# A mixture-of-experts block in fp32r: the transposes of the next tile's rows move from the down-projection to the last up-projection chunk

## The reference

```python
w = weights[subjects]                           # one 64x64 map of 8 for each of 64 batches
xf = einsum('bct,bcd->bdt', x, w).reshape(-1, 512)         # 4096 tokens, 512 wide
probs = softmax(xf @ gate_w.T); top_p, top_i = top_k(probs, 2)     # 8 experts
h = silu(einsum('nc,efc->enf', xf, fc1)) * einsum('nc,efc->enf', xf, fc2)    # f: 352
out_e = einsum('enf,ecf->enc', h, proj)
y = einsum('ne,enc->nc', combine, out_e)        # combine holds top_p at top_i
shared = silu(xf @ shared_fc1.T) * (xf @ shared_fc2.T) @ shared_proj.T       # f: 1408
return x + y + sigmoid(xf @ shared_gate_w.T) * shared
```

## Time and profile before

| | |
|---|---|
| median of three runs | 1295.43 us (1293.08 to 1296.06) |
| profiled execution: span from first to last instruction | 1294.0 us |
| TensorE busy | 1277.8 us, 99% of the span |
| TensorE weight loads (PEld) | 1104.3 us, 85% |
| VectorE, ScalarE, GpSimd busy | 757.2, 442.1, 230.9 us |
| HBM traffic | 172 GB/s over the span |

### The profile page before, as it was taken

How to read it: one execution, slowest core, us unless ns; L and a number is a source line. 1 busy time by engine, 2 the same in 40 slices (tenths; PEclk the granted TensorE clock), 3 DMA queues, 4 the chain that set the end, 5 groups by cost and what they waited for, 6 DMA issues and landing times.

```text
span 1294.0 us, 20330 instructions
## 1 busy us (share of the span) xinstructions
PE 1277.8 (99%) x7150; PEld 1104.3 (85%) x7150; DVE 757.2 (59%) x1285; ACT 442.1 (34%) x744; POOL 230.9 (18%) x336
## 2 busy tenths in 40 slices
PE   6999999999999999999999999999999999999998
PEld 5888888888888989999999999998888888888886
DVE  5444443459645777777687677767535435445444
ACT  4323231121012666566566565555101101101100
POOL 4121220000001222212211221110122122122031
PEclk9999999999999999999999999999999999999999
DMA  9454544201235767777768766756152351351342
GB/s 317 125 196 144 203 126 163 106 33 66 98 124 186 273 248 257 267 260 261 264 238 279 269 224 242 254 212 220 60 163 60 103 162 48 114 162 43 120 130 65
DMA packets 84491, 222.72 MB, mean 172 GB/s; under 512 B 8578, under 2 KB 8706, under 8 KB 79458
## 3 DMA queue, kind: packets, MB, share of 16 engines
q1 hardware_dynamic: 73650, 186.77, 40.4%
q0 software_dynamic: 10800, 35.40, 10.0%
HBM read 169.97 MB, written 52.17 MB: 172 GB/s over the span
## 4 chain that ended last, share of the span: by engine, by line
PE 95%; DMA 2%; DVE 1%; issue 1%; SPq 1%; ACT 0%; POOLq 0%; POOL 0%; DVEq 0%
PE bank_h L644 60%; PE bank_o L644 29%; PE bank_t L634 2%; PE bank_t L644 2%; PE bank_t L591 1%; DMA rawp<-ewp 1%; PE bank_o L601 1%; PE bank_h L601 1%; DMA rawp<-swp 0%; DMA picked<-slot_rows,idx_stage 0%; PE bank_t L752 0%; DVE res L1333 0%; PE bank_h L853 0%; SPq L316 0%; DVE w_lo L1362 0%
## 5 line engine op out<-in xcount | busy, mean ns | idle before, releaser
L644 PE MATMUL bank_h<-x_hi,w_hi 128*128 128x256 f32 (+1 forms) x1480 | 499.6, 338 | 3.6 <-DVE x_lo L1370 2.8
L644 PE MATMUL bank_h<-x_hi,w_lo 128*128 128x256 f32 (+1 forms) x1480 | 493.3, 333 | 0.0
L644 PE MATMUL bank_h<-x_lo,w_hi 128*128 128x256 f32 (+1 forms) x1480 | 492.8, 333 | 0.0
L644 PEld LDWEIGHTS bank_h<-x_hi,w_hi 128*128 128x128 f32 x1480 | 273.4, 185 | 31.1 <-issue 4.7
L644 PEld LDWEIGHTS bank_h<-x_hi,w_lo 128*128 128x128 f32 x1480 | 273.3, 185 | 27.4
L644 PEld LDWEIGHTS bank_h<-x_lo,w_hi 128*128 128x128 f32 x1480 | 273.5, 185 | 26.4
L959 ACT ACTIVATE g_sb<-bank_h 128x512 f32<-128x512 f32 x88 | 52.6, 598 | 580.0 <-PE bank_h L644 580.0
L644 PE MATMUL bank_o<-wp_hi,h_hi 128*128 128x512 f32 (+1 forms) x565 | 229.4, 406 | 0.0
L1289 DVE TENSOR_TENSOR h_sb<-bank_h,g_sb 96x256 f32<-96x256 f32 (+1 forms) x184 | 101.3, 550 | 218.4 <-ACT g_sb L959 193.8
L644 PE MATMUL bank_o<-wp_lo,h_hi 128*128 128x512 f32 (+1 forms) x565 | 228.7, 405 | 0.0
L644 PE MATMUL bank_o<-wp_hi,h_lo 128*128 128x512 f32 (+1 forms) x565 | 227.5, 403 | 0.0
(11 more groups left out here) (154 smaller groups left out, 1134.3 us busy)
## 6 DMA issues: line engine op xcount, KB each, us to landing
raw<-ew SPq DMA_DIRECT2D x39, 1408.0 KB, 7.4
rawp<-ewp SPq DMA_DIRECT2D x39, 512.0 KB, 7.9
slot_rows<-res SPq DMA_DIRECT2D x32, 512.0 KB, 4.6
xt_in<-xf_transposed SPq DMA_DIRECT2D x15, 1024.0 KB, 8.3
picked<-x SPq DMA_DIRECT2D x32, 256.0 KB, 3.2
xf_rows<-rows SPq DMA_DIRECT2D x32, 256.0 KB, 3.3
res<-x SPq DMA_DIRECT2D x8, 1024.0 KB, 5.3
partial_rows<-res SPq DMA_DIRECT2D x8, 1024.0 KB, 4.2
```

The source lines that it names most:

```text
L644: mm = pe.matmul(dst, a, m, start=(first and i == 0), stop=(last and i == 2))
```

## The change

The eight (or four) transposes of the next tile's rows leave the down-projection. They stand in the last up chunk of the tile, one after every second pass from the second on. The wait for the gathered rows moves with them, to just ahead of that chunk. Nothing else changes: the queues of ScalarE, VectorE, GpSimd and SyncE are the same row by row. Single steps keep their transposes where they were.

```diff
--- before.py
+++ after.py
@@ -778,27 +778,36 @@
                         transpose_rows(ex, 0, k, rows[:, k, :])
                 shared_row(0, BLOCKS - 1, r)
 
-            def up_product(i, u, j, h, k, start, stop):
+            def up_product(i, u, j, h, k, start, stop, small=None):
 
                 f0, fn = FCH[j]
                 a = u * E_UP + k * 2 * F + h * F + f0
                 return product(bank_h[j][0:fn, h * TS:(h + 1) * TS], (w12_hi[:, a:a + fn], w12_lo[:, a:a + fn]),
-                               (x_hi[:, k, 0:TS], x_lo[:, k, 0:TS]), start, stop)
-
-            def whole_chunk(i, u, j):
+                               (x_hi[:, k, 0:TS], x_lo[:, k, 0:TS]), start, stop, small)
+
+            def whole_chunk(i, u, j, row_tiles=0):
                 at_least(pe, ex.h_mul, 3 * (i - 1) + j + 1)
                 for h in range(2):
                     for k in range(KC):
-                        m = up_product(i, u, j, h, k, k == 0, k == KC - 1)
+
+                        def small(pas, at=3 * (KC * h + k)):
+                            q, odd = divmod(at + pas, 2)
+                            if odd and q < row_tiles * KC:
+                                transpose_rows(ex, 2 * (i + 1), q // KC, rows[:, 2 * (1 - u) + q // KC, :], (q % KC,),
+                                               3 - row_tiles)
+
+                        m = up_product(i, u, j, h, k, k == 0, k == KC - 1, small)
                 m.then_inc(ex.h_full, 1)
 
-            def expert_stage1(i, u):
+            def expert_stage1(i, u, row_tiles=0, loaded=0):
                 pe.wait_ge(ex.x_lo, 2 * (i + 1))
                 pe.wait_ge(ex.w_lo, PIECES * i + KC)
                 for j in range(3):
-                    whole_chunk(i, u, j)
-
-            def expert_stage2(i, u, row_tiles):
+                    if j == 2 and row_tiles:
+                        pe.wait_ge(ex.rows_loaded[1 - u], loaded)
+                    whole_chunk(i, u, j, row_tiles if j == 2 else 0)
+
+            def expert_stage2(i, u):
 
                 pe.wait_ge(ex.w_lo, PIECES * (i + 1))
                 if isinstance(i, int) and i == 0:
@@ -812,22 +821,15 @@
                             fn = FCH[k][1]
                             w = slice(u * E_DOWN + k * C, u * E_DOWN + (k + 1) * C)
 
-                            def small(pas, at=3 * (2 * r + k)):
-                                q = at + pas
-                                if ks != (2,) and q < row_tiles * KC:
-                                    transpose_rows(ex, 2 * (i + 1), q // KC, rows[:, 2 * (1 - u) + q // KC, :], (q % KC,),
-                                                   3 - row_tiles)
-
                             m = product(bank_o[r][:, :], (h_hi[0:fn, k, c], h_lo[0:fn, k, c]),
-                                        (wp_hi[0:fn, w], wp_lo[0:fn, w]), k == 0, k == 2, small)
+                                        (wp_hi[0:fn, w], wp_lo[0:fn, w]), k == 0, k == 2)
                         if ks == (2,):
                             m.then_inc(ex.o_full, 1)
 
             def whole_step(i, u, loaded, row_tiles=2):
 
-                expert_stage1(i, u)
-                pe.wait_ge(ex.rows_loaded[1 - u], loaded)
-                expert_stage2(i, u, row_tiles)
+                expert_stage1(i, u, row_tiles, loaded)
+                expert_stage2(i, u)
 
             def single_up(i):
 
@@ -879,9 +881,9 @@
                     if k == 0:
                         single_transpose(i, g)
                 single_down(i)
-                whole_chunk(i + 1, 1, 2)
                 pe.wait_ge(ex.rows_loaded[0], loaded_next)
-                expert_stage2(i + 1, 1, 2)
+                whole_chunk(i + 1, 1, 2, 2)
+                expert_stage2(i + 1, 1)
 
             whole_step(0, 0, 32)
             whole_step(1, 1, 48, 1)
@@ -895,7 +897,7 @@
                 whole_step(TAIL + 2 * it, 0, 32 * it + 16 * TAIL + 32)
                 whole_step(TAIL + 1 + 2 * it, 1, 32 * it + before + 64)
             expert_stage1(XT - 1, 0)
-            expert_stage2(XT - 1, 0, 0)
+            expert_stage2(XT - 1, 0)
 
             shared_stage1(1, 0)
             pe.wait_ge(ex.o_kept, 2 * XT)
```

## The result

The changed kernel takes 1298.31 us (median of ten runs, 1296.83 to 1300.78) against 1294.03 us before (ten runs, 1293.08 to 1296.41): 4.3 us more, ratio 1.0029, 95% interval 1.0019 to 1.0038. The forecast was 1299.9 us with 0.70 on slower by over 0.2%. The profiled execution's span is 1298.9 us.

The account below looks back on a forecast made before the run. TensorE was taken to bound the kernel (busy 1277.8 of 1294.0 us). Terms -0.9 + 4.9 + 0.5 = +4.5 us gave a span of 1298.5, plus 1.4 for the median: 1299.9 us, range 1295.0 to 1302.8 (8 in 10).

Parts of the forecast that it names:

- Price of a transpose: 220 moved transposes, now after 256-column matmuls, cost 0.112 instead of 0.116 us each: -0.9 us, ends -2.0 to +2.0.
- Waits in the tiles after a single: TensorE waits 0.82 us for `x_lo` at the next tile after single-and-whole steps, six of seven times: +4.9 us.
- so its wait stays as it is: First of seven single-and-whole steps: late weights, not the gate, set its limit, so no added wait there.
- First tile: Tile 0, two pieces of `wp` ahead of `x_lo` on VectorE: one new TensorE wait, 4.27 + 0.32 - 4.13 = +0.5 us.
- Plain tiles: No new wait: `x_lo` ready 3.5 us after the last up chunk, needed at 4.13; `h_lo` cover left 0.6 us.
- The rows' wait: The wait for gathered rows stands 2.8 us earlier, ahead of 24 matmuls; release and use move together, so no cost.
- The sum: Whole kernel: -0.9 + 4.9 + 0.5 = +4.5 us, forecast 1299.9 us, slower by 0.35%.
- Cheap transposes: Rival: shorter 96-column weight load makes a moved transpose cost 0.090, -5.7 us against waits of +5.4: 1295.1 us; chance 0.12.
- No new wait: Rival: VectorE's chain to `x_lo` is held by earlier weight splits, not the gate; only price term left, 1294.5 us; chance 0.06.
- Dear transposes: Rival: behind a 256-column matmul a transpose's load is partly uncovered, up to 0.14 us: +5.3 instead of -0.9, 1306.1 us; chance 0.05.
- The estimate from the Trainium skill: Load time proportional to columns (107 and 80 ns); with load as limit, moved transposes 0.027 us cheaper, 5.9 us in all.

Follow-up runs that it names:

- the undisturbed ones: Two further traces of the unaltered kernel before, each a single execution: 1292.16 and 1293.89 us, expert stage 481.24 and 481.31 us.
- e7: The kernel before with only the wait for the gathered rows moved ahead of the last up chunk; 1294.62 us, ratio 1.0004.
- e3: The changed kernel, but in whole steps the transposes stand in the middle up chunk (128-column weights), not the last; 1299.57 us, ratio 1.0037.
- e8: The kernel before with the transposes in one row between the last up chunk and the down matmuls, behind the raising of `h_full`; 1292.39 us, ratio 0.9980.
- e4: The changed kernel with weight splits on VectorE and ScalarE put earlier in the first tile and tiles after a single; 1293.3 us, ratio 0.9991.

## Why the prediction was right, and where it was off

- *Price of a transpose*, -0.9 us: last chunk and twelve down matmuls add up to 204.0 us over the 32 whole tiles before and to 203.0 after, by their starts, so -1.0 us. The price is 0.110 against the 0.112 taken; that alone would be about -1.2, and the slower twelve in the tiles after a single give 0.2 of it back.
- *Waits in the tiles after a single*, 0.82 us each: measured 0.77, or 0.80 with the slower twelve, and the mechanism to 0.01 us (C + 4.63 in both kernels). But seven have it, not six. The step that failed is "so its wait stays as it is": I took the wait of the earlier trace rows (0.94 us between starts, and 0.10 behind it) as fixed, and it differs from trace to trace; in both traces of the change that tile has the same 0.77 as the others. Whether the change itself keeps the late weights away there stays open. Against the first trace this is a gain of 0.3 us, against the undisturbed ones a loss of 0.8.
- *First tile*, +0.5 us: measured 0.24 (429.60 is C + 4.27 where 4.13 is due, and 0.10 behind it). The chain was right but for 0.05, and the delay behind `x_lo` mis-sized: 0.15, not 0.32. The timeline of the first tile, after:

```profile
425.33 0.40 PE L644 MATMUL bank_o<-wp_hi,h_hi 128*128 128x512 f32 x1
...
427.07 1.28 DVE L1411 TENSOR_TENSOR wp_lo<-rawp,wp_hi 128x512 fp32r<-128x512 f32 x2
...
428.27 1.28 DVE L1301 TENSOR_TENSOR x_lo<-bank_t,x_hi 128x512 fp32r<-128x512 f32 x2
...
429.60 0.39 PE L644 MATMUL bank_h<-x_hi,w_hi 128*128 128x256 f32 x1
...
429.82 0.28 PE L644 MATMUL bank_h<-x_lo,w_hi 128*128 128x256 f32 x1
```

`x_lo` ends at 429.55 and the matmul starts at 429.60. Outside the loops the waits are constants, and the trace shows no register operation ahead of this matmul. I had the row of the loop and used it for both.
- *Plain tiles*, nothing: right, and with the play forecast. A plain tile after, to read against the earlier trace rows:

```profile
804.01 0.38 ACT L1034 ACTIVATE g_sb<-bank_h 96x256 f32<-96x256 f32 x1 [2.28 <-PE bank_h L644]
...
804.29 1.07 ACT L915 ACTIVATE x_hi<-bank_t 128x512 fp32r<-128x512 f32 x2
...
805.20 0.42 DVE L1295 TENSOR_TENSOR h_lo<-h_sb,h_hi 96x256 fp32r<-96x256 f32 x1
...
805.54 1.28 DVE L1301 TENSOR_TENSOR x_lo<-bank_t,x_hi 128x512 fp32r<-128x512 f32 x2
...
807.92 0.28 PE L644 MATMUL bank_h<-x_hi,w_hi 128*128 128x256 f32 x1
```

ScalarE takes `x_hi` straight behind the gate (in the earlier trace rows VectorE waited 0.69 us for it) and `x_lo` ends at 806.82; C is 803.81, so C + 3.01, forecast C + 3.2, with the next tile at C + 4.11.
- *The rows' wait*, nothing: right (e7).
- *The sum*, +4.5 us: the stage rose by 3.6 us against the first trace and by 4.7 against the two others, the median by 4.3. That the sum came out near the 4.7 of the undisturbed traces is in part luck, since errors cancel: the seventh wait adds 0.8, while the first tile (0.3), the size of the other six waits (6 x 0.05 = 0.3) and the price (0.1) take off 0.7. The time of 1299.9 us was 1.6 us too high, and 1.4 of that is the base: 1295.43 us was the median of three runs, and ten runs gave 1294.03. The range's ends, added up (1295.4 + 2.4 and + 7.9), would be 1297.8 and 1303.3, so its upper end of 1302.8 was written 0.5 too low.
- *The rivals.* Cheap transposes: refuted by the price of 0.110 (0.090 was its number), and its reason by e3 (0.111 behind 128-wide weights, 0.110 behind 96-wide). No new wait: refuted by the first trace after. Dear transposes: refuted by the same 0.110. The estimate from the Trainium skill ("TensorE: Matmul & The Clock Gate", LDWEIGHTS) does not apply to this stretch, because by e3 the load is not what limits it here. Of the rule itself bear out the difference between the two widths (26 ns, 27 by the rule), but not the durations (189 and 163 ns, 107 and 80 by the rule).

## What to carry to other kernels

Filler work that is moved ahead of a signal delays all that the signal releases, even when the busy engine does the same work in the same total time: follow the chain from that signal to the point where the busy engine next needs it, and compare with what the engine has left to do in between. Here 0.9 us moved from behind `h_full` to ahead of it, and the seven tiles that had only 0.1 us of play (ready at C + 4.95, reached at C + 5.06) made nearly the whole loss; the first tile made 0.24 us. Put the filler directly behind the signal (e8), or use the idle time that the later signal leaves the other engine (e4).

## What the runs showed of the hardware

- A 128x128 float32 transpose costs TensorE about 0.11 us wherever it is put, though its row shows 0.27: 0.108 to 0.112 in a row of eight (e8), 0.110 and 0.111 behind 256-column matmuls with 96 and 128 columns of weights (the change, e3), 0.116 between 512-column matmuls (before).
- Where several waits stand ahead of an instruction in a loop, and their values are worked out in registers, their order matters: with the wait that arrives last put last, the matmul started 0.05 us after `x_lo` and not 0.22, seven times, 1.1 us of the stage. Where the values were constants (the first tile), the same edit made it 0.15 and not 0.05.
- One execution's trace can hold a wait that others of the same kernel do not: 482.4, 481.3 and 481.2 us for the same stage, 1.1 us apart where the change made 4.7.
